# ViT tower on one core: squares of the patch embedding weighted on ACT, folded on POOL, one PE product per tile, with constants and clearing moved

## The chip, the cores and the metric

The kernel runs on 1 core of one Trainium2 chip. The metric is device time in microseconds for one execution of the whole tower. The time before is 2521.09 us, the median of 3 runs (2516.54 to 2526.69).

## What is computed

Thirty-two images of 3x112x112 become 49 patch tokens each, plus a class token, so 1600 tokens of 192 numbers. Four pairs of mixer and feed-forward layers follow (a state-space scan, attention, mixtures of experts). The change touches the tokeniser, which is a shifted-patch embedding: each patch is read together with four shifted copies, the row is layer-normalised and projected:

```python
h = _L0_tok_ref(x, L0_tok_ln_weight, L0_tok_ln_bias, L0_tok_proj_weight, L0_tok_proj_bias)
h = jnp.concatenate([jnp.broadcast_to(cls_tok, (h.shape[0], 1, h.shape[2])), h], axis=1)
h = h + _L0_attn_ref(_layernorm(h, axis=-1), ...)
```

The layer norm of a patch needs the mean and the mean square over its window, each pixel counted as often as the five copies read it (its share). The kernel gets both from matrix products over the pixels: the mean as a 193rd column of the projection, the mean square as a column of its own.

## The kernel before, in words

`embed` (from L121) works in 16 tiles of 100 tokens (two images). A tile's pixels lie as 8 chunks of 120 rows by 100 tokens. Four buffers (DEPTH = 4) hold pixels and squares in turn.

SP's queue loads three small tables, 8 chunks of shifted weights (`wshift`, L168), and then one tile of pixels after another (L176); from the fifth on, a pixel load waits until PE has finished the tile that used the buffer four tiles earlier (`multiplied`). Behind every second one of these it loads a quarter of the packed constants (L180), and the block ends with a wait for all four quarters.

DVE folds each weight chunk over its 5 shifts (L194, L198), and PE forms two bias rows from the same chunks (L267, L270). Then, for each tile, ACT squares the 800 pixels per row in one instruction (L252). PE waits for the squares, multiplies the 8 pixel chunks by the 193 folded columns (L279) and the 8 chunks of squares by the one column `share` (L282). A product in f32 shows as two instructions, so a tile has 16 and 16. DVE's `centre` (L208 to L210) takes the tile out of PSUM; after every fourth tile `variance` (L215 to L217), ACT's root and `scale` (L222, L225, L229) finish four tiles. PE may begin a tile only when `centre` of four tiles earlier has run (`stored`). POOL does nothing in this block.

`zero_spare` (from L1711) is a block of its own behind it: DVE casts two constants to bf16 (L1720, L1721), POOL clears a tile (L1725), SP stores it to the spare rows of `sums` (L1730) and waits for the store. Then `layer0_mixer` normalises (L325 and following, over DVE, POOL and ACT), projects and enters its scan (`bilinear_scan`, L558 to L675). The two bf16 constants are first used by the experts of layer 1's feed-forward. `layer1_mixer` begins with POOL copying token tiles (L1265) for PE.

Blocks follow each other: every engine ends its part before any engine begins the next block.

Of the kernel before, what the change touches and what calls it, by code (L numbers as in the profile page):

```python
# [32 lines left out]
WROWS = 120  # L33
# [31 lines left out]
class Tower:  # L65


    def __init__(self, nc, stack, args, where):
        self.nc, self.stack, self.args, self.sems, self.tensors = nc, stack, args, 0, 0
        sb = self.sbuf  # L70
        self.h = sb("h", [TILE, TILES, DIM])
        self.x = sb("x", [TILE, TILES, DIM])
        self.xT = sb("xT", [128, 2, TOKENS + 2 * TILE])
        self.psum = stack.enter_context(nc.psum_tensor("banks", [128, 8 * 512], F32))
        self.bank = [self.psum[:, 512 * i:512 * (i + 1)] for i in range(8)]
        self.old, self.theirs, self.new, self.mine = ExitStack(), [], ExitStack(), []
        self.bn = sb("bn", [TILE, TILES, 6])
        self.mv = sb("mv", [TILE, TILES, 2])
        self.loaded = self.sem("constants_loaded", lasting=True)
        self.passed = self.sem("passed", lasting=True)  # L80

        self.tables = {k: nc.dram_tensor(f"table{k}", (TOKENS, LINE + 2 * k), F32, kind="Internal").ap() for k in (2, 4)}
        self.behind = sb("behind", [TILE, TILE], dtype=BF16)
        self.every = sb("every", [TILE, 128], dtype=BF16)
        self.sums = nc.dram_tensor("sums", (TOKENS + SPARE, DIM), F32, kind="Internal").ap()
        self.consts = sb("consts", list(args["consts"].shape))
        self.w = {}
        for name, (at, shape) in where.items():
            self.w[name] = columns_of(self.consts, at, shape)

# [42 lines left out]
def embed(t):  # L133
# [4 lines left out]
    with ExitStack() as st:  # L138
# [4 lines left out]
        gain = t.sbuf("gain", [WROWS, 2, WCHUNKS, SHIFTS], st)  # L143
        share = t.sbuf("share", [WROWS, WCHUNKS], st)
        onesr = t.sbuf("onesr", [WROWS, TILE], st)
        pbias = t.sbuf("pbias", [1, DIM], st)
        rows = t.sbuf("rows", [TILE, 2, DIM], st)
        stats = t.sbuf("pstats", [TILE, TILES, 2], st)
# [7 lines left out]
        finished = t.sem("finished")  # L156
        raw, fixed = t.bank[4:4 + DEPTH], t.bank[2:4]
        args = t.args
        width = t.consts.shape[1]

        with t.block() as block:
            @block.sync
            def _(sp):
                sp.dma_start(gain[:], args["ln_gain"]).then_inc(small_in, 16)
                sp.dma_start(share[:], args["share"]).then_inc(small_in, 16)
                sp.dma_start(pbias[:], args["patch_bias"]).then_inc(small_in, 16)
                for c in range(WCHUNKS):
                    sp.dma_start(wshift[:, c], args["w_patch"][:, c]).then_inc(weights_in[c], 16)  # L168
                for n in range(TILES):
                    if n == DEPTH:  # L170
                        sp.wait_ge(rows_done, 1)
                        for image in range(2):
                            sp.dma_start(rows[SEQ * image:SEQ * image + 1, 1, :], args["cls"][0]).then_inc(cls_in, 16)
                    if n >= DEPTH:
                        sp.wait_ge(multiplied, n - DEPTH + 1)
                    sp.dma_start(pixels[:, n % DEPTH], args["pixels"][n]).then_inc(pixels_in[n % DEPTH], 16)  # L176
                    part = (n - DEPTH) // 2
                    if n >= DEPTH and n % 2 and part < CONST_PARTS:
                        at = slice(width * part // CONST_PARTS, width * (part + 1) // CONST_PARTS)
                        sp.dma_start(t.consts[:, at], args["consts"][:, at]).then_inc(t.loaded, 16)  # L180
                sp.wait_ge(t.loaded, 16 * CONST_PARTS)

            @block.vector
            def _(dve):
# [1 line left out]
                nc.vector.memset(onesr[:], 1.0).then_inc(ones_done, 1)  # L186
                one(nc.vector.memset(t.xT[0:HALF + 1, :, TOKENS:], 0.0))
                one(nc.vector.memset(t.xT[HALF:HALF + 1, :, TOKENS:], 1.0))
                dve.wait_ge(small_in, 48)
                nc.vector.tensor_copy(wsum[:, :, DIM:DIM + 1], share[:].unsqueeze(2)).then_inc(share_done, 1)  # L190

                for c in range(WCHUNKS):
# [46 lines left out]
            @block.scalar  # L239
            def _(act):  # L240
                nc.scalar.preload_act_table(ACT.Sqrt)

                def root(g):
                    at = slice(DEPTH * g, DEPTH * (g + 1))
                    act.wait_ge(var_done, g + 1)
                    nc.scalar.activation(var[:, 4, at], var[:, 3, at], ACT.Sqrt).then_inc(root_done, 1)

                for n in range(TILES):
                    act.wait_ge(pixels_in[n % DEPTH], 16 * (n // DEPTH) + 16)
                    if n >= DEPTH:  # L250
                        act.wait_ge(multiplied, n - DEPTH + 1)
                    nc.scalar.activation(squares[:, n % DEPTH], pixels[:, n % DEPTH], ACT.Square).then_inc(squared, 1)  # L252
                    if n % DEPTH == 2 and n > DEPTH:
                        root(n // DEPTH - 1)
                root(TILES // DEPTH - 1)

            @block.tensor
            def _(pe):
                pe.sem_inc(stored, DEPTH)
                pe.wait_ge(ones_done, 1)  # L260
                pe.wait_ge(small_in, 48)

                nc.tensor.matmul(fixed[1][0:TILE, 0:DIM], onesr[0:1, :], pbias[:], start=True, stop=False)
                for c in range(WCHUNKS):
                    pe.wait_ge(weights_in[c], 16)
                    for s in range(SHIFTS):
                        nc.tensor.matmul(fixed[1][0:TILE, 0:DIM], gain[:, 1, c, s:s + 1].to_broadcast([WROWS, TILE]),  # L267
                                         wshift[:, c, s, :], start=False, stop=(c == WCHUNKS - 1 and s == SHIFTS - 1))
                    pe.wait_ge(wsum_done, SHIFTS * (c + 1))
                    last = nc.tensor.matmul(fixed[0][0:TILE, 0:DIM], onesr[:], wsum[:, c, 0:DIM],  # L270
                                            start=(c == 0), stop=(c == WCHUNKS - 1))
                last.then_inc(bias_done, 1)
                pe.wait_ge(share_done, 1)
                for n in range(TILES):
                    u = n % DEPTH
                    pe.wait_ge(squared, n + 1)
                    pe.wait_ge(stored, n + 1)
                    for c in range(WCHUNKS):
                        nc.tensor.matmul(raw[u][0:TILE, 0:DIM + 1], pixels[:, u, c, :], wsum[:, c, :],  # L279
                                         start=(c == 0), stop=(c == WCHUNKS - 1))  # L280
                    for c in range(WCHUNKS):
                        last = nc.tensor.matmul(raw[u][0:TILE, DIM + 1:DIM + 2], squares[:, u, c, :],  # L282
                                                share[:, c:c + 1], start=(c == 0), stop=(c == WCHUNKS - 1))
                    last.then_inc(multiplied, 1)


# [234 lines left out]
def bilinear_scan(t, u, rate, coef, bc, direct, gain, y):  # L521
# [7 lines left out]
    with ExitStack() as st:  # L529
# [12 lines left out]
        lasts = [max(j for j in range(jobs) if group(j) == g) for g in range(2)]  # L542

        with t.block() as block:
            @block.tensor
            def _(pe):
                pe.sem_inc(summed, SLOTS)
# [694 lines left out]
def layer1_mixer(t):  # L1242

    nc, w = t.nc, t.w
    with ExitStack() as st:
# [12 lines left out]
        with t.block() as block:  # L1258
            @block.gpsimd
            def _(pool):  # L1260
                with pool.Fori(0, TILES // 2) as i:
                    for u in range(2):
                        pool.wait_ge(projected, 2 * i + u + 1)
# [442 lines left out]

def rounds(engine, times):
    return engine.Fori(0, times) if times > 1 else nullcontext(0)


def zero_spare(t):  # L1711

    nc = t.nc
    with ExitStack() as st:
        zeros = t.sbuf("zeros", [128, SUBS, DIM], st)
        zeros_done, zeroed = t.sem("zeros_done"), t.sem("zeroed")
        with t.block() as block:
            @block.vector
            def _(dve):
                nc.vector.tensor_copy(t.behind[:], t.w["behind"])  # L1720
                nc.vector.tensor_copy(t.every[:], t.w["all"])  # L1721

            @block.gpsimd
            def _(pool):
                nc.gpsimd.memset(zeros[:], 0.0).then_inc(zeros_done, 1)  # L1725

            @block.sync
            def _(sp):
                sp.wait_ge(zeros_done, 1)
                sp.dma_start(t.sums[TOKENS:TOKENS + SPARE].rearrange("(s p) d -> p s d", p=128), zeros[:]).then_inc(zeroed, 16)  # L1730
                sp.wait_ge(zeroed, 16)


def experts(t, name, src, dst, lhs, router, count, picks, func, gated, norm=None, own_gain=False, out=None, keep_sum=None, biased=False, capacity=None):
# [661 lines left out]
def tower(nc, args, out, where):  # L2396
    with ExitStack() as stack:
        t = Tower(nc, stack, args, where)
        embed(t)
        zero_spare(t)  # L2400
        layer0_mixer(t)
        layer0_ffn(t)
        layer1_mixer(t)
# [73 lines left out]
def layout(inputs):  # L2477
# [21 lines left out]
    a["w_patch"] = np.ascontiguousarray(wide[..., :DIM])  # L2499
    a["ln_gain"] = np.ascontiguousarray(wide[..., DIM:].transpose(0, 3, 1, 2))  # L2500
    a["share"] = np.ascontiguousarray((count / PATCH_DIM).astype(np.float32).reshape(WCHUNKS, WROWS).T)
    a["patch_bias"] = f["L0_tok_proj_bias"].reshape(1, DIM)
    a["cls"] = f["cls_tok"].reshape(1, 1, DIM)
    a["c_ident"] = np.eye(128, dtype=np.float32)
# [96 lines left out]
```

## Time and profile before

| | |
|---|---|
| median of 3 runs | 2521.09 us |
| the profiled execution's own time | 2526.45 us |
| its span, first to last instruction | 2524.6 us |
| mean granted TensorE clock | 0.859 |
| PE busy | 2005.6 us (79%) |
| DVE busy | 1189.0 us (47%) |
| ACT busy | 890.3 us (35%) |
| POOL busy | 843.8 us (33%) |

Times are microseconds from the span's start unless ns is written. PE is TensorE's matrix products, PEld its weight loads, which overlap with them, DVE is VectorE, ACT ScalarE, POOL GpSimd, SP the queue that issues most transfers. The engine shares are averages over stages with different limits, so a stage is read by itself: its timeline, its busy time per window, and what each engine waited for.

### The profile page before, as it was taken

Reading aid. Unit: us, or ns where it says so; the run is one execution under the profiler, and the core shown is the slowest. Engines: PE = TensorE matmul, PEld = TensorE weight load, DVE = VectorE, ACT = ScalarE, POOL = GpSimd, SP = SyncE. Lnnn points to the kernel's source line nnn. Section 1 sums busy time; section 2 is a strip of 40 time slices with the busy share of each in tenths; the row PEclk is TensorE's granted clock in tenths of the full one; section 3 lists DMA queues with packets and bytes.
Section 4 is the critical chain, followed back from the end, with each engine's and each line's share of the span. In section 5 each row is a group of like instructions: output and inputs, shape, how many; then the busy total and the mean of one; then the engine's idle time right before and its main releaser. Section 6 shows DMA issues by size and latency. Waiting matters only on the chain. (4 is left out here: it accounts for less than half of the span.)

```text
span 2524.6 us, 42132 instructions
## 1 busy us (share of the span) xinstructions
PE 2005.6 (79%) x13338; PEld 1484.1 (59%) x13338; DVE 1189.0 (47%) x2907; ACT 890.3 (35%) x1860; POOL 843.8 (33%) x759
## 2 busy tenths in 40 slices
PE   9755777987995994985995567777499938999998
PEld 8511223665764883664983222224399837999987
DVE  4348995243563113563113799998222243222222
ACT  1247784133233332342224644553222122211211
POOL 0203552012111553001552267663234312443443
PEclk9757997876896995895997789999599957999999
DMA  7100000000004871003871000000377626777774
GB/s 217 31 0 1 0 0 1 0 0 6 1 0 122 237 206 35 1 0 106 225 205 26 0 1 0 0 0 1 113 223 221 170 69 191 224 222 224 221 201 113
DMA packets 95935, 228.18 MB, mean 90 GB/s; under 512 B 22481, under 2 KB 60948, under 8 KB 87540
## 3 DMA queue, kind: packets, MB, share of 16 engines
q1 hardware_dynamic: 64564, 188.81, 23.4%
q0 software_dynamic: 31296, 38.48, 8.4%
q8 instruction: 34, 0.56, 0.1%
q14 instruction: 41, 0.34, 0.0%
HBM read 199.63 MB, written 27.62 MB: 90 GB/s over the span
## 5 line engine op out<-in xcount | busy, mean ns | idle before, releaser
L1964 PE MATMUL banks<-wt,hid 128*128 128x192 f32 x1932 | 331.7, 327 | 0.4
L1964 PEld LDWEIGHTS banks<-wt,hid 128*128 128x128 f32 x1932 | 311.8, 190 | 1.5 <-issue 0.6
L1866 POOL DMA_INDIRECT xblock<-table,take x169 | 167.6, 992 | 370.7 <-DVE gate L2149 193.8
L1939 PE MATMUL banks<-xTblock,wt 128*128 128x256 f32 (+1 forms) x1464 | 268.6, 341 | 1.7 <-ACT xTblock L2022 1.2
L2162 DVE TENSOR_TENSOR hid<-sa,banks 128x512 f32<-128x512 f32 (+1 forms) x183 | 105.9, 579 | 340.1 <-ACT sa L2043 337.3
L2043 ACT ACTIVATE sa<-banks 128x512 f32<-128x512 f32 (+1 forms) x183 | 93.3, 510 | 481.5 <-PE banks L1950 476.6
L1939 PEld LDWEIGHTS banks<-xTblock,wt 128*128 128x128 f32 x1464 | 237.6, 194 | 23.7 <-issue 1.9
L742 PE MATMUL banks<-g,consts 128*128 128x400 f32 x384 | 184.7, 571 | 60.1 <-DVE g L881 56.1
L850 POOL TENSOR_TENSOR w<-u,spreadB 128x400 f32<-128x400 f32 x192 | 192.9, 1034 | 87.0 <-ACT spreadB L821 87.0
L1871 POOL DMA_INDIRECT sums<-yblock,put x96 | 152.7, 1591 | 170.5 <-issue 98.6
L875 DVE TENSOR_TENSOR_SCAN s<-banks,w 128x400 f32<-128x400 f32 x192 | 187.7, 977 | 4.2 <-POOL w L850 4.2
L2177 DVE TENSOR_SCALAR yblock<-banks,gate 128x192 f32<-128x192 f32 x129 | 49.4, 414 | 235.2 <-PE banks L1964 204.3
L742 PEld LDWEIGHTS banks<-g,consts 128*128 128x128 f32 x384 | 61.0, 197 | 168.4 <-DVE g L881 167.2
L633 POOL TENSOR_TENSOR w<-u,r 128x400 f32<-128x400 f32 x96 | 99.0, 1033 | 175.4 <-ACT r L607 163.4
L805 ACT ACTIVATE banks<-rate,coef 128x392 f32 x192 | 113.2, 591 | 117.8 <-DVE s L875 117.8
L1950 PE MATMUL banks<-xTblock,wt 64*128 64x256 f32 (+1 forms) x1464 | 143.3, 342 | 0.0
L1871 POOL DMA_INDIRECT out<-yblock,put x65 | 103.6, 1594 | 115.0 <-issue 56.5
L1950 PEld LDWEIGHTS banks<-xTblock,wt 64*128 64x128 f32 x1464 | 116.1, 187 | 22.9 <-issue 12.1
L881 DVE TENSOR_TENSOR g<-s,banks 128x400 f32<-128x400 f32 x192 | 103.3, 540 | 0.0
L1943 PE MATMUL banks<-xTblock,wt 128*128 128x256 f32 (+1 forms) x480 | 94.7, 349 | 2.2 <-ACT xTblock L2022 1.3
L656 DVE TENSOR_TENSOR_SCAN s<-banks,w 128x400 f32<-128x400 f32 x96 | 93.8, 977 | 0.1
L1926 PE MATMUL banks<-consts,xblock 128*128 128x128 f32 x338 | 61.5, 296 | 38.7 <-DMA xblock<-table,take 38.6
(379 smaller groups left out, 3455.5 us busy)
## 6 DMA issues: line engine op xcount, KB each, us to landing
wt<-L3f_packed SPq DMA_DIRECT2D x41, 1152.0 KB, 5.6
wt<-L_packed SPq DMA_DIRECT2D x60, 576.0 KB, 4.6
wt<-L3f_packed SPq DMA_DIRECT2D x41, 576.0 KB, 5.4
wt<-L3m_packed SPq DMA_DIRECT2D x20, 1152.0 KB, 5.4
wt<-L_packed SPq DMA_DIRECT2D x20, 675.0 KB, 4.2
wt<-L3m_packed SPq DMA_DIRECT2D x20, 577.0 KB, 5.4
pixels<-pixels SPq DMA_DIRECT2D x16, 375.0 KB, 4.8
wshift<-w_patch SPq DMA_DIRECT2D x8, 450.0 KB, 11.9
```

The costliest lines, as they stand in the source:

```text
L633: nc.gpsimd.tensor_tensor(w1[:, j % SLOTS, :], u[:, group(j), at], r[:, j % SLOTS, :], ALU.mult).then_inc(w1_done, 1)
L742: nc.tensor.matmul(acc[g][0:parts, 0:CHUNK], ident[0:parts, 0:parts], g_[:, j % SLOTS, :], start=(n == 0), stop=(n == STATES - 1)).then_in ...
L805: nc.scalar.activation(rest, rate[:, g, at].rearrange("p (b t) -> p b t", t=SEQ)[:, :, 1:SEQ], ACT.Exp, scale=coef[:, g, n:n + 1]).then_in ...
L850: nc.gpsimd.tensor_tensor(w2[:, j % SLOTS, :], u[:, g, at], spreadB[:, n % 2, :], ALU.mult).then_inc(bu_done, 1)
L875: nc.vector.tensor_tensor_scan(s[:, j % SLOTS, :], decays[j % DECAYS], w2[:, j % SLOTS, :], 0.0, ALU.mult, ALU.add).then_inc(s_done, 1)
L881: nc.vector.tensor_tensor(g_[:, j % SLOTS, :], s[:, j % SLOTS, :], bankC[(j // groups) % 2][0:parts, 0:CHUNK], ALU.mult).then_inc(g_done, 1)
L1866: nc.gpsimd.indirect_dma_start(x[:, b % 2, q - column_of_block[b], :], None, table, bass.IndirectOffsetOnAxis(take[:, q:q + 1], 0)).then_i ...
L1871: nc.gpsimd.indirect_dma_start(sums, bass.IndirectOffsetOnAxis(put[:, q:q + 1], 0), y[:, b % 2, q - column_of_block[b], :], None, compute_ ...
L1939: nc.tensor.matmul(bank[:, n * j:n * (j + 1)], wt[:, v, cols(base, 2 * p + j)], xT[:, v, 0, 0:n], start=(j == 0), stop=False, skip_group_c ...
L1950: last = nc.tensor.matmul(bank[:, n * j:n * (j + 1)], wt[half, v, cols(REST_AT, 2 * p + j)], xT[half, v, 1, 0:n], start=False, stop=True, ...
L1964: last = nc.tensor.matmul(bankY[s], hid[:, m, 128 * s:128 * (s + 1)], wt[:, v, DOWN_AT + DIM * m:DOWN_AT + DIM * (m + 1)], start=(m == 0 a ...
L2162: nc.vector.tensor_tensor(hid[:, 2 * p:2 * p + 2, 0:n], sa[:, (PAIRS * v + p) % 2, 0:2 * n].rearrange("p (m n) -> p m n", m=2), second[:, ...
```

## The change

The squares are weighted before they are summed. ACT squares each chunk by itself with a scale per row, the root of `share`, so 8 instructions replace one. POOL adds the 8 weighted chunks in three halving additions (4+4 chunks, 2+2, 1+1). PE multiplies the one folded chunk by a column of ones: one product per tile in place of eight. PE now waits for the pixels ahead of the 193-column products and for POOL's sum ahead of the last one.

The clearing of spare rows goes inside `embed`, ahead of the weight loads in SP's queue; the two casts go to POOL at the start of `layer1_mixer`; the block `zero_spare` disappears. Of the constants, the first part (up to the array `first`, 737 of the columns by the arrays' shapes) is loaded behind the ninth pixel tile and awaited at the block's end; the rest is loaded in four parts behind the last pixel tile and awaited by SP in the block of `bilinear_scan`.

```diff
             def _(sp):
                 sp.dma_start(gain[:], args["ln_gain"]).then_inc(small_in, 16)
                 sp.dma_start(share[:], args["share"]).then_inc(small_in, 16)
+                sp.dma_start(root_share[:], args["root_share"]).then_inc(small_in, 16)
                 sp.dma_start(pbias[:], args["patch_bias"]).then_inc(small_in, 16)
+                sp.wait_ge(zeros_done, 1)
+                sp.dma_start(t.sums[TOKENS:TOKENS + SPARE].rearrange("(s p) d -> p s d", p=128), zeros[:]).then_inc(zeroed, 16)
...
                     if n >= DEPTH:
                         sp.wait_ge(multiplied, n - DEPTH + 1)
+                        sp.wait_ge(squared, n - DEPTH + 1)
                     sp.dma_start(pixels[:, n % DEPTH], args["pixels"][n]).then_inc(pixels_in[n % DEPTH], 16)
-                    part = (n - DEPTH) // 2
-                    if n >= DEPTH and n % 2 and part < CONST_PARTS:
-                        at = slice(width * part // CONST_PARTS, width * (part + 1) // CONST_PARTS)
-                        sp.dma_start(t.consts[:, at], args["consts"][:, at]).then_inc(t.loaded, 16)
-                sp.wait_ge(t.loaded, 16 * CONST_PARTS)
+                    if n == 2 * DEPTH:
+                        sp.dma_start(t.consts[:, 0:early], args["consts"][:, 0:early]).then_inc(t.loaded, 16)
+                for part in range(CONST_PARTS):
+                    at = slice(early + late * part // CONST_PARTS, early + late * (part + 1) // CONST_PARTS)
+                    sp.dma_start(t.consts[:, at], args["consts"][:, at]).then_inc(t.loaded_late, 16)
+                sp.wait_ge(t.loaded, 16)
+                sp.wait_ge(zeroed, 16)
...
                     if n >= DEPTH:
-                        act.wait_ge(multiplied, n - DEPTH + 1)
-                    nc.scalar.activation(squares[:, n % DEPTH], pixels[:, n % DEPTH], ACT.Square).then_inc(squared, 1)
+                        act.wait_ge(added_up, n - DEPTH + 1)
+                    for c in range(WCHUNKS):
+                        last = nc.scalar.activation(squares[:, n % DEPTH, c, :], pixels[:, n % DEPTH, c, :], ACT.Square, scale=root_share[:, c:c + 1])
+                    last.then_inc(squared, 1)
...
+            @block.gpsimd
+            def _(pool):
+                one = Steps(pool, pool_step)
+                nc.gpsimd.memset(zeros[:], 0.0).then_inc(zeros_done, 1)
+                for n in range(TILES):
+                    u = n % DEPTH
+                    pool.wait_ge(squared, n + 1)
+                    if n >= DEPTH:
+                        pool.wait_ge(multiplied, n - DEPTH + 1)
+                    one(nc.gpsimd.tensor_tensor(halved[:], squares[:, u, 0:4, :], squares[:, u, 4:8, :], ALU.add))
+                    one(nc.gpsimd.tensor_tensor(halved[:, 0:2, :], halved[:, 0:2, :], halved[:, 2:4, :], ALU.add))
+                    nc.gpsimd.tensor_tensor(total[:, u, :], halved[:, 0, :], halved[:, 1, :], ALU.add).then_inc(added_up, 1)
+                    pool.wait_ge(added_up, n + 1)
...
-                    pe.wait_ge(squared, n + 1)
+                    pe.wait_ge(pixels_in[u], 16 * (n // DEPTH) + 16)
                     pe.wait_ge(stored, n + 1)
...
-                    for c in range(WCHUNKS):
-                        last = nc.tensor.matmul(raw[u][0:TILE, DIM + 1:DIM + 2], squares[:, u, c, :],
-                                                share[:, c:c + 1], start=(c == 0), stop=(c == WCHUNKS - 1))
+                    pe.wait_ge(added_up, n + 1)
+                    last = nc.tensor.matmul(raw[u][0:TILE, DIM + 1:DIM + 2], total[:, u, :], onesr[:, 0:1], start=True, stop=True)
                     last.then_inc(multiplied, 1)
...
+            @block.sync
+            def _(sp):
+                sp.wait_ge(t.loaded_late, 16 * CONST_PARTS)
...
             def _(pool):
+                nc.gpsimd.tensor_copy(t.behind[:], t.w["behind"])
+                nc.gpsimd.tensor_copy(t.every[:], t.w["all"])
                 with pool.Fori(0, TILES // 2) as i:
```

## Rows read from the trace of the kernel before

**Rows 1.** Windows: stretch, busy time (instructions) per engine, PEclk, DMA share, GB/s.

```profile
25.00:90.00 65.00, 64.79 (x514) 64.70 (x512) 20.60 (x84) 12.57 (x17) 0.00 (x0) 1.00 0.51 158
```

**Rows 2.** Timeline, PE's weight loads in one tile: start, length, group.

```profile
45.19 2.56 PEld L279 LDWEIGHTS banks<-wsum,pixels 120*100 120x100 f32 x16
47.75 1.56 PEld L282 LDWEIGHTS banks<-share,squares 120*100 120x100 f32 x16
...
49.23 2.56 PEld L279 LDWEIGHTS banks<-wsum,pixels 120*100 120x100 f32 x16
```

**Rows 3.** Timeline from the last work of embed to the mixer's first.

```profile
92.90 1.13 DVE L229 BATCH_NORM_STATS2 bn<-h 100x6 f32<-100x192 f32 x4
94.30 0.42 POOL L1725 MEMSET zeros<- 128x384 f32 x1 [93.86 <-POOLq L108]
...
98.27 1.28 ACT L409 ACT_TABLE_LOAD   x1 [6.93 <-PEq L108]
```

**Rows 4.** Groups by shape, POOL's tensor-by-tensor operations: busy us, mean ns.

```profile
L850 POOL TENSOR_TENSOR w<-u,spreadB 128x400 f32<-128x400 f32 x192 | 192.9, 1034 | 87.0 <-ACT spreadB L821 87.0
...
L1394 POOL TENSOR_TENSOR h<-h,x 100x192 f32<-100x192 f32 x2 | 1.2, 592 | 9.4 <-DVE x L1628 9.4
```

**Rows 5.** Timeline, POOL additions and products beside DVE, in two later layers.

```profile
987.76 6.66 POOL L1399 TENSOR_TENSOR h<-h,wproj 100x3072 f32<-100x3072 f32 x1 [1.44 <-DMA wproj<-L_proj]
...
990.12 4.33 DVE L1591 TENSOR_SCALAR norm<-norm 100x24 f32<-100x24 f32 x1
...
1411.83 1.40 DVE L2376 SCALAR_TENSOR_TENSOR plain<-w__231,e 128x1200 f32<-128x1200 f32 x1
...
1411.99 3.81 POOL L2330 TENSOR_TENSOR u<-rate,xc 128x1200 f32<-128x1200 f32 x1 [49.90 <-DVE rate L2371]
...
1449.40 2.71 POOL L2330 TENSOR_TENSOR u<-rate,xc 128x1200 f32<-128x1200 f32 x1 [4.23 <-DVE rate L2371]
```

**Rows 6.** Groups by shape, DVE in 205 to 360 us, beside POOL's products of L633.

```profile
L662 DVE TENSOR_TENSOR g<-s,banks 128x400 f32<-128x400 f32 x77 | 43.0, 558 | 0.1
```

**Rows 7.** Timeline, the scan's start: ACT hands over to POOL.

```profile
208.33 0.52 ACT L607 ACTIVATE r<-den 128x400 f32<-128x400 f32 x1
...
209.22 2.03 POOL L633 TENSOR_TENSOR w<-u,r 128x400 f32<-128x400 f32 x2 [94.09 <-ACT r L607]
```

**Rows 8.** Groups by shape, ACT instructions with one operand per row.

```profile
L1309 ACT ACTIVATE probs<-scores,low 100x100 f32<-100x100 f32 x16 | 5.9, 370 | 9.2 <-DVE low L1329 9.2
...
L1002 ACT ACTIVATE sq<-rate,consts 128x800 f32<-128x800 f32 x4 | 3.5, 951 | 0.0
```

**Rows 9.** Timeline, the four instructions of L1002 back to back.

```profile
186.00 3.52 ACT L1002 ACTIVATE sq<-rate,consts 128x800 f32<-128x800 f32 x4
```

**Rows 10.** Timeline, the head of embed.

```profile
1.26 0.36 SPq L165 DMA_DIRECT2D share<-share  x1
...
1.96 3.67 SPq L168 DMA_DIRECT2D wshift<-w_patch  x8
...
6.36 0.32 DVE L194 TENSOR_SCALAR wsum<-wshift,gain 120x192 f32<-120x192 f32 x1 [2.97 <-DMA wshift<-w_patch]
```

**Rows 11.** DMA issues: count, KB each, median us to landing.

```profile
pixels<-pixels SPq DMA_DIRECT2D x16, 375.0 KB, 4.8
...
consts<-consts SPq DMA_DIRECT2D x2, 1337.5 KB, 8.0
```

**Rows 12.** Timeline, POOL's first work in layer 1's mixer.

```profile
526.43 0.64 POOL L1265 COPY xtile<-xT 97x200 f32 x2 [2.83 <-PEq L1269]
```

**Rows 13.** Windows in layer 1's mixer (columns as in Rows 1).

```profile
526.80:530.50 3.70, 3.67 (x19) 3.61 (x20) 0.00 (x0) 0.52 (x1) 0.27 (x1) 0.50 0.00 0
531.10:533.00 1.90, 1.90 (x19) 1.90 (x19) 0.36 (x1) 0.50 (x1) 0.35 (x1) 0.92 0.00 0
```

**Rows 14.** Timeline, the same weight loads in those two windows.

```profile
529.93 0.61 PEld L1281 LDWEIGHTS banks<-consts,xtile 96*100 96x100 f32 x2
...
532.70 0.33 PEld L1281 LDWEIGHTS banks<-consts,xtile 96*100 96x100 f32 x2
```

More of the change, by code:

```diff
@@ L79, in __init__ @@
         self.loaded = self.sem("constants_loaded", lasting=True)
+        self.loaded_late = self.sem("constants_loaded_late", lasting=True)
         self.passed = self.sem("passed", lasting=True)
@@ L86, in __init__ @@
         self.consts = sb("consts", list(args["consts"].shape))
-        self.w = {}
+        self.w, self.where = {}, where
         for name, (at, shape) in where.items():
@@ L145, in embed @@
         onesr = t.sbuf("onesr", [WROWS, TILE], st)
+        root_share = t.sbuf("root_share", [WROWS, WCHUNKS], st)
+        halved = t.sbuf("halved", [WROWS, WCHUNKS // 2, TILE], st)
+        total = t.sbuf("total", [WROWS, DEPTH, TILE], st)
+        zeros = t.sbuf("zeros", [128, SUBS, DIM], st)
+        zeros_done, zeroed, added_up, pool_step = (t.sem(n) for n in ("zeros_done", "zeroed", "added_up", "pool_step"))
         pbias = t.sbuf("pbias", [1, DIM], st)
@@ L158, in embed @@
         args = t.args
-        width = t.consts.shape[1]
+        early = t.where["first"][0]
+        late = t.consts.shape[1] - early
         with t.block() as block:
@@ L188, in _ @@
                 one(nc.vector.memset(t.xT[HALF:HALF + 1, :, TOKENS:], 1.0))
-                dve.wait_ge(small_in, 48)
+                dve.wait_ge(small_in, 64)
                 nc.vector.tensor_copy(wsum[:, :, DIM:DIM + 1], share[:].unsqueeze(2)).then_inc(share_done, 1)
@@ L249, in _ @@
                     act.wait_ge(pixels_in[n % DEPTH], 16 * (n // DEPTH) + 16)
+                    if n == 0:
+                        act.wait_ge(small_in, 64)
                     if n >= DEPTH:
-                        act.wait_ge(multiplied, n - DEPTH + 1)
-                    nc.scalar.activation(squares[:, n % DEPTH], pixels[:, n % DEPTH], ACT.Square).then_inc(squared, 1)
+                        act.wait_ge(added_up, n - DEPTH + 1)
+                    for c in range(WCHUNKS):
+                        last = nc.scalar.activation(squares[:, n % DEPTH, c, :], pixels[:, n % DEPTH, c, :], ACT.Square, scale=root_share[:, c:c + 1])
+                    last.then_inc(squared, 1)
                     if n % DEPTH == 2 and n > DEPTH:
@@ L260, in _ @@
                 pe.wait_ge(ones_done, 1)
-                pe.wait_ge(small_in, 48)
+                pe.wait_ge(small_in, 64)
                 nc.tensor.matmul(fixed[1][0:TILE, 0:DIM], onesr[0:1, :], pbias[:], start=True, stop=False)
@@ L1708, in rounds @@
     return engine.Fori(0, times) if times > 1 else nullcontext(0)
[L1711 to L1731, printed above, removed]
 def experts(t, name, src, dst, lhs, router, count, picks, func, gated, norm=None, own_gain=False, out=None, keep_sum=None, biased=False, capacity=None):
@@ L2399, in tower @@
         embed(t)
-        zero_spare(t)
         layer0_mixer(t)
@@ L2501, in layout @@
     a["share"] = np.ascontiguousarray((count / PATCH_DIM).astype(np.float32).reshape(WCHUNKS, WROWS).T)
+    a["root_share"] = np.sqrt(a["share"])
     a["patch_bias"] = f["L0_tok_proj_bias"].reshape(1, DIM)
```

## Prediction
> **What bounds the kernel now.** I read four views in this order: the page's table of engines, the windows of the first 100 us, the timeline of one tile and of the passage into the mixer, and the groups by shape for prices. The page says that PE is busiest, but the change touches only the embedding and the block behind it, so their own rows decide. While the tiles run, PE and its weight loads are busy throughout, at granted clock 1.00, while DVE has 20.60 us of work in 65, ACT 12.57 and POOL none [rows 1]. So PE sets the pace there. One tile shows its two parts: the 16 loads of the 193-column products start at 45.19, the 16 of the one-column products at 47.75, the next tile at 49.23 [rows 2]. A tile takes 4.04 us: 2.56 for the first part and 1.48 for the second, which gives just one column. Sixteen tiles take 64.6 us. DVE's last instruction of embed ends at 94.03, the clearing block begins at 94.30, the mixer at 98.27 [rows 3]: 3.97 us for a block in which no engine does much.
>
> **What PE saves.** Of the second part two loads of 16 stay: 2 x 1.48/16 = 0.19 us. The tile becomes 2.56 + 0.19 = 2.75 us, 16 tiles 44.0, so -20.6 us if PE still sets the pace. For that, ACT, POOL, DVE and the pixel ring must each need less than 2.75 us a tile.
>
> **ACT.** An instruction of 100x100 with one operand per row takes 0.370 us; four in a row of 0.951 each take 3.52 together, so each overlaps the next by 0.095 [rows 8, 9]. Eight squares: 7 x 0.275 + 0.37 = 2.3 us. That fits, with 0.45 to spare, and ACT can run up to four tiles ahead. It costs nothing; PE's products hide it.
>
> **POOL.** Additions of 400 and 192 elements took 1034 and 592 ns [rows 4]: 2.125 ns an element and 184 fixed. So 400, 200 and 100 elements take 1.03, 0.61 and 0.40 us: 2.04 a tile. Between them stand three waits of POOL on its own result, which no row shows. From below a wait costs nothing; from above it costs what ACT's handover to POOL took, 209.22 - 208.85 = 0.37 [rows 7]. A handover inside one engine should be nearer the low end: I take 0.15, so 2.5 us a tile (2.04 to 3.15).
>
> **POOL beside DVE.** The same product of 128x1200 took 2.71 us alone and 3.81 where a DVE instruction with two SBUF inputs had begun 0.16 before it; and a DVE TENSOR_SCALAR of 24 elements, begun at 990.12, ended at 994.45, just after POOL's addition ended at 994.42 [rows 5]. So whichever comes second waits out the other. DVE's products of an SBUF with a PSUM operand were not held: 558 ns beside POOL [rows 6]. In embed the two-input ones are L215, L216 and the four of L225, with L217 a TENSOR_SCALAR: 7 of the 21 DVE instructions of four tiles (84/4). Each may wait for one addition, on average 0.68 us: at most 4.8 us per four tiles on top of DVE's own 5.2 [rows 1], 10.0 in all against PE's 11.0. In return they hold POOL. If they make up some 2 of the 5.2 us, an estimate, that is 0.5 a tile at most, so POOL needs 2.5 to 3.0, PE 2.75. PE is still the likelier bound, as many of these instructions fall into POOL's pauses, but DVE will be late at the end: I take +1.5 us (0 without holds, 4.8 with all of the last four tiles' holds).
>
> The open one is L209, the negation of one element, once per tile. By the 24-element row it is held too, 16 times more; this is in the upper half of my bounds. The Trainium skill's page "GPSIMD Engine Reference", section "Specifications", limits contention to DVE instructions with two SBUF inputs or in a two-port mode. By it L209 would be held only if one element ran in such a mode, and the +1.5 would be nearer 1.0; no row tells.
>
> **The pixel ring.** A slot is refilled after `multiplied`: issue 0.3, landing 4.8 [rows 11], ACT 2.3, POOL 2.5, PE's last product 0.2 make 10.1 us against 4 x 2.75 = 11.0. It fits. The early constants (737 columns x 512 B = 0.38 MB) are as much as one pixel tile and add one such transfer in the ring's slack. SP's extra wait for `squared` is met whenever `multiplied` is.
>
> **The head.** Ahead of the weight loads SP gets two more issues, `root_share` and the store of zeros, at 0.36 each as for `share`: +0.7, and their bytes ahead of the first weight chunk. POOL clears its tile in 0.42 [rows 3] right at the start, before SP asks. DVE's folding starts on the first chunk's landing (6.36 [rows 10]) and everything up to the first tile hangs on it. I take +1.0 (0.4 if the issues overlap with the landing; 2.8 if the store adds 2 us).
>
> **The block removed, the rest.** -4.0 us; at the least -3.5 if the passage between blocks gets longer. The casts in `layer1_mixer` stand ahead of POOL's first copy, for which PE waits: two copies of 200 elements took 0.64 together [rows 12], the casts have 100 and 128, so +0.5 (0 to 0.64). The late constants, four parts of 1337 KB less 0.38 MB, about 5.1 MB, flow from the last pixel load on. At the 158 GB/s of rows 1 they take 32 us and end some 20 us into the mixer. Their wait is SP's alone, in the scan's block, which began 110 us after the mixer (208.33 against 98.27 [rows 3, 7]); SP has nothing queued behind it. Cost nothing, and if that cover went, the scan would start late by the remainder.
>
> **Sum.** -20.6 + 1.5 + 1.0 - 4.0 + 0.5 = -21.6 us. The profiled execution would go from 2526.45 to 2504.9. It lies 5.4 above the median, so the median of runs would go from 2521.1 to **2499.5 us**. Best case: -20.6 + 0 + 0.4 - 4.0 + 0 = -24.2.
>
> **Rivals.**
> *POOL becomes the bound.* At waits of 0.37 and half of the holds a tile takes 3.15 + 0.25 = 3.4 us, 16 tiles 54.4: -10.2 + 1.5 + 1.0 - 4.0 + 0.5 = -11.2, 2510; with every hold 3.65 and -7.2, 2514; at waits of 0.25 it is 2.79 + 0.25 = 3.04 and -17.0, 2504. For it: the prices lie close to PE's 2.75. Against: both must come out high, and POOL starts a tile ahead.
> *The pixels or constants are late.* If landings take 6.5 us in place of 4.8, the ring needs 11.8 per four tiles, 2.95 each, 47.2 in all: -18.4, 2503. If the mixer waited for the late constants, 10 to 20 us would come back, 2510 to 2520; nothing that it reads before the scan stands in the late part.
> *Slower: PE at its lower clock level in the tiles.* A busy PE is not enough for the higher level: in 526.8 to 530.5 it was busy 3.67 of 3.70 us at a granted 0.50 (1.2 GHz), and its weight loads took 0.61 there against 0.33 just after, at 0.92 [rows 13, 14]. At that ratio, 1.85, a tile takes 5.1 us and 16 take 81.4: +16.8 + 1.0 - 4.0 + 0.5 = +14.3, 2535. The point from which it decides is a tile of 4.2 us, where what the loop loses eats the removed block. Against it: the level held at 1.00 through all 65 us with the same 193-column products [rows 1], and what goes are the thin ones, so PE gets denser.
>
> **How the numbers follow.** PE-bound as summed 0.65; POOL the bound 0.23, about half of it short of 0.5%; late transfers 0.07; the lower clock 0.05. Half a per cent, 12.6 us, is what a measurement here can tell from no change, so faster means below 2508.5. Faster: 0.62 + 0.12 + 0.05 = 0.79; same: 0.03 (scatter of three runs) + 0.11 + 0.02 = 0.16; slower 0.05. The range goes from the best case with the scatter of the runs before (5 below their median), 2497 - 9, to the dearer POOL case, so 2488 to 2512.
>
> **What would show it.** Right: PE's weight loads start tiles 2.75 us apart, PE busy without gaps in them; embed ends near 75, and the mixer's first table load comes at 75 to 76 in place of 98.27; eight ACT instructions of about 0.37 a tile; POOL's adds at 1.03, 0.61, 0.40 and the longer ones beside L225; no later stage changed. Wrong: PE waiting for `total` in every tile (POOL the bound), ACT or PE waiting for pixels, a granted clock under 1.00 in 26 to 70, or a mixer that starts on time and loses the gain before the scan.

## The result, and the profile after

The changed kernel takes 2499.68 us (median of 4 runs, 2496.99 to 2501.28), the kernel before 2518.82 (4 runs, 2515.87 to 2526.69). The ratio is 0.9918, with a 95% interval of 0.9903 to 0.9934, so the gain is 17 to 24 us. The prediction was 2499.5, a gain of 21.6 from the earlier median of 2521.1. A second timing, beside the experiments, gave 2498.85 against 2520.14, ratio 0.9904 (0.9866 to 0.9942).

The profiled execution of the changed kernel has its own time of 2501.28 us, a span of 2499.4 and a mean granted clock of 0.86. First the timeline, cut to the lines that answer to [rows 2, 3, 7, 10], with others between them left out, as in the timelines further on (start, length, group, and in brackets the idle time before it and what ended it).

```profile
2.86 3.91 SPq L178 DMA_DIRECT2D wshift<-w_patch  x8
...
7.37 0.32 DVE L207 TENSOR_SCALAR wsum<-wshift,gain 120x192 f32<-120x192 f32 x1 [3.78 <-DMA wshift<-w_patch]
...
25.69 2.63 PEld L310 LDWEIGHTS banks<-wsum,pixels 120*100 120x100 f32 x16
25.77 1.03 POOL L283 TENSOR_TENSOR halved<-squares 120x400 f32<-120x400 f32 x1 [24.63 <-ACT squares L268]
26.88 0.61 POOL L284 TENSOR_TENSOR halved<-halved 120x200 f32<-120x200 f32 x1
27.56 0.39 POOL L285 TENSOR_TENSOR total<-halved 120x100 f32<-120x100 f32 x1
...
42.58 2.56 PEld L310 LDWEIGHTS banks<-wsum,pixels 120*100 120x100 f32 x16
44.00 2.26 ACT L268 ACTIVATE squares<-pixels,root_share 120x100 f32<-120x100 f32 x8 [1.16 <-DMA pixels<-pixels]
45.13 0.33 PEld L313 LDWEIGHTS banks<-onesr,total 120*100 120x100 f32 x2
45.38 2.56 PEld L310 LDWEIGHTS banks<-wsum,pixels 120*100 120x100 f32 x16
...
67.48 0.40 POOL L285 TENSOR_TENSOR total<-halved 120x100 f32<-120x100 f32 x1
...
70.51 0.25 PE L313 MATMUL banks<-onesr,total 120*100 120x1 f32 x2
...
72.56 1.41 DVE L238 SCALAR_TENSOR_TENSOR h<-h,pvar,rows 100x192 f32<-100x192 f32 x4
73.88 1.13 DVE L242 BATCH_NORM_STATS2 bn<-h 100x6 f32<-100x192 f32 x4
75.28 1.28 ACT L439 ACT_TABLE_LOAD   x1 [2.97 <-PEq L109]
...
182.99 1.28 ACT L627 ACT_TABLE_LOAD   x1 [12.00 <-DVE banks L674]
...
781.55 1.28 ACT L2044 ACT_TABLE_LOAD   x1
937.41 1.28 ACT L439 ACT_TABLE_LOAD   x1 [13.13 <-PEq L109]
```

Read it downwards. The first weight chunk is folded at 7.37 where it was 6.36, and the first tile's loads begin at 25.69. A tile starts 2.80 us after the one before it (42.58 to 45.38), where it was 4.04; the first part is unchanged at 2.56, and the two loads of `total` take 0.25 (45.13 to 45.38) in place of the second part. ACT's eight squares take 2.26 us together. POOL's three additions follow each other after 0.08 and 0.07 us (26.80 to 26.88, 27.49 to 27.56). DVE's last instruction of `embed` ends at 75.01 (73.88 + 1.13), and the mixer's first ACT instruction comes 0.27 later: there is no block between them any more. The mixer starts 98.27 - 75.28 = 22.99 us earlier. The scan's table load comes 182.99 - 75.28 = 107.71 us behind it. In the kernel before it stood equally far behind, as this line shows against the 98.27 of [rows 3]:

```profile
205.98 1.28 ACT L593 ACT_TABLE_LOAD   x1 [12.00 <-DVE banks L640]
```

So nothing of the gain is lost before the scan, and the new wait in its block costs nothing. The windows of the changed kernel say what PE and the transfers did (columns as in [rows 1]):

```profile
25.00:70.00 45.00, 45.00 (x290) 45.00 (x289) 26.10 (x83) 34.51 (x126) 32.81 (x48) 1.00 0.63 195
65.00:70.00 5.00, 5.00 (x34) 5.00 (x33) 3.53 (x15) 0.54 (x2) 2.05 (x3) 1.00 1.00 420
70.00:74.00 4.00, 0.77 (x7) 0.68 (x5) 2.75 (x12) 0.20 (x1) 0.00 (x0) 1.00 1.02 426
```

PE is busy through all 45 us at granted clock 1.00, so it still sets the pace, with ACT at 77% and POOL at 73% close under it. The late constants run at 420 GB/s and are nearly through by 74. Last the groups by shape of the changed kernel in 0 to 80 us, and the DVE groups of the kernel before in 25 to 94 that answer to them.

```profile
L268 ACT ACTIVATE squares<-pixels,root_share 120x100 f32<-120x100 f32 x128 | 35.8, 364 | 27.4 <-DMA pixels<-pixels 27.2
L283 POOL TENSOR_TENSOR halved<-squares 120x400 f32<-120x400 f32 x16 | 16.8, 1047 | 31.4 <-ACT squares L268 24.6 <-POOL total L285 5.3 <-issue 1.2
L284 POOL TENSOR_TENSOR halved<-halved 120x200 f32<-120x200 f32 x16 | 9.7, 608 | 1.3
L238 DVE SCALAR_TENSOR_TENSOR h<-h,pvar,rows 100x192 f32<-100x192 f32 x16 | 8.9, 616 | 0.1
L285 POOL TENSOR_TENSOR total<-halved 120x100 f32<-120x100 f32 x16 | 6.3, 395 | 1.3
L222 DVE TENSOR_SCALAR pvar<-pstats 100x1 f32<-100x1 f32 x16 | 2.5, 154 | 0.5
L228 DVE TENSOR_TENSOR pvar<-pstats 100x4 f32<-100x4 f32 x4 | 1.9, 472 | 0.0
L230 DVE TENSOR_SCALAR pvar<-pvar 100x4 f32<-100x4 f32 x4 | 1.3, 320 | 0.1
```

```profile
L225 DVE SCALAR_TENSOR_TENSOR h<-h,pvar,rows 100x192 f32<-100x192 f32 x16 | 5.6, 415 | 0.1
L209 DVE TENSOR_SCALAR pvar<-pstats 100x1 f32<-100x1 f32 x16 | 2.5, 153 | 0.6
L217 DVE TENSOR_SCALAR pvar<-pvar 100x4 f32<-100x4 f32 x4 | 0.7, 170 | 0.1
L215 DVE TENSOR_TENSOR pvar<-pstats 100x4 f32<-100x4 f32 x4 | 0.6, 156 | 0.0
```

The same DVE instructions stand in both, at other lines: 415 became 616 ns, 156 became 472, 170 became 320, and the negation of one element stayed at 153 and 154. The spans of the two profiles differ by 25.2 us while the medians differ by 19.1 and, in the second timing, 21.3. That difference is taken up with the experiments.

### The profile page after: what moved, and what is told of

Read it like the earlier page. It is cut to its first block and busy times, and to the rows that moved or that the text cites. A ratio compares the mean times of both kernels' runs of the same rounds, so it can differ in the third digit from the quotient of the medians.

```text
span 2499.4 us, 41869 instructions
## 1 busy us (share of the span) xinstructions
PE 1984.9 (79%) x13114; PEld 1463.7 (59%) x13114; DVE 1194.3 (48%) x2905; ACT 911.7 (36%) x1972; POOL 876.6 (35%) x809
## 5 line engine op out<-in xcount | busy, mean ns | idle before, releaser
L1884 POOL DMA_INDIRECT sums<-yblock,put x96 | 152.7, 1591 | 168.4 <-issue 93.4
```

The source lines that it names most:

```text
L1884: nc.gpsimd.indirect_dma_start(sums, bass.IndirectOffsetOnAxis(put[:, q:q + 1], 0), y[:, b % 2, q - column_of_block[b], :], None, compute_ ...
```

## The experiments

All are edits of the changed kernel, but the last one, which is the kernel before profiled again. To compare stages without the head, I use the stretch from the first tile's weight load to the mixer's first table load: 98.27 - 24.93 = 73.34 us before and 75.28 - 25.69 = 49.59 after.

**The squares undone** (`e2_old_squares`): ACT squares the tile in one instruction again, PE has its eight one-column products, POOL adds nothing.

```diff
-                    for c in range(WCHUNKS):
-                        last = nc.scalar.activation(squares[:, n % DEPTH, c, :], pixels[:, n % DEPTH, c, :], ACT.Square, scale=root_share[:, c:c + 1])
-                    last.then_inc(squared, 1)
+                    nc.scalar.activation(squares[:, n % DEPTH], pixels[:, n % DEPTH], ACT.Square).then_inc(squared, 1)
...
-                    pe.wait_ge(added_up, n + 1)
-                    last = nc.tensor.matmul(raw[u][0:TILE, DIM + 1:DIM + 2], total[:, u, :], onesr[:, 0:1], start=True, stop=True)
+                    pe.wait_ge(squared, n + 1)
+                    for c in range(WCHUNKS):
+                        last = nc.tensor.matmul(raw[u][0:TILE, DIM + 1:DIM + 2], squares[:, u, c, :],
+                                                share[:, c:c + 1], start=(c == 0), stop=(c == WCHUNKS - 1))
```

> Only the squares are undone: one ACT instruction per tile, no POOL adds, eight one-column products; the constants, the clearing and the waits stay as in the change. Theory (PE's products were the gain): a tile takes 4.04 us again, 16 x 1.24 = 19.8 us more, the mixer's first table load at 95.1, the whole time about 2519. Rival (the earlier constants among the pixel loads slowed the tiles, and moving them was the gain): tiles near 3 us, the mixer at 76 to 82.

It took 2512.68 us. Its timeline:

```profile
45.15 2.56 PEld L298 LDWEIGHTS banks<-wsum,pixels 120*100 120x100 f32 x16
47.70 1.56 PEld L302 LDWEIGHTS banks<-share,squares 120*100 120x100 f32 x16
49.19 0.92 PEld L298 LDWEIGHTS banks<-wsum,pixels 120*100 120x100 f32 x6
...
94.25 1.28 ACT L429 ACT_TABLE_LOAD   x1 [2.96 <-PEq L109]
```

The tile is back at 4.04 us and the mixer at 94.25. From the first tile (24.89) to the mixer it is 69.36, so the squares are worth 69.36 - 49.59 = 19.77 us, and what remains to the kernel before, 73.34 - 69.36 = 3.98, is the block. The start 0.85 earlier than forecast lies in the head, whose scatter is treated below. The whole time is 6 us under the 2519 forecast; how far a single time can be trusted is treated there too.

**The block put back** (`e1_block`): the clearing, its store and the two casts return to a block behind `embed`.

```diff
+def zero_spare(t):
...
+                nc.vector.tensor_copy(t.behind[:], t.w["behind"])
+                nc.vector.tensor_copy(t.every[:], t.w["all"])
...
+                nc.gpsimd.memset(zeros[:], 0.0).then_inc(zeros_done, 1)
...
-                sp.wait_ge(zeroed, 16)
+                sp.wait_ge(t.loaded_late, 16 * CONST_PARTS)
...
-                nc.gpsimd.tensor_copy(t.behind[:], t.w["behind"])
-                nc.gpsimd.tensor_copy(t.every[:], t.w["all"])
```

> The block of clearing and casts stands behind embed again, the store of zeros no longer ahead of the weights, the casts no longer in layer 1; the squares stay as in the change. Theory (the block cost 3.97 us by itself, the store some 0.45 at the head): tiles stay 2.80 us apart, embed's last DVE instruction ends at 74.5 in place of 75.01, the mixer's first table load comes at 78.5 to 79 in place of 75.28. If the casts on POOL cost layer 1's mixer 0.5 us, its stretch between the two table loads (84.30 us in the changed kernel) goes to 83.8; if not it stays at 84.2 or more. Rival (the block was hidden, the whole shift came from the tiles): the mixer at 75.3.

It took 2499.16 us. Its timeline:

```profile
75.49 0.42 POOL L1755 MEMSET zeros<- 128x384 f32 x1 [9.09 <-remote]
77.63 0.39 SPq L1760 DMA_DIRECT2D sums<-zeros  x1
...
80.05 1.28 ACT L435 ACT_TABLE_LOAD   x1 [9.04 <-PEq L109]
```

DVE's last instruction of `embed` ended at 73.70 here, 0.8 ahead of the forecast; that is the head again, as it lies 49.32 us behind the first tile (24.38), like the changed kernel's (75.01 - 25.69). The block brings the wait for its store back, but the mixer is later than I expected: the casts read late constants, so this kernel must wait for all of them ahead of the block, which the expectation left out. From 73.70 to 75.49 are 1.79 us, where the passage into the block took 0.27 before (94.03 to 94.30, [rows 3]), so the wait is 1.5 of them; from the clearing to the mixer it is 4.56, against 98.27 - 94.30 = 3.97. The 0.6 that this is longer by lies between the clearing and the issue of its store, 77.63 - 75.49 = 2.14 us here and 95.82 - 94.30 = 1.52 before; why was not tried. Of the casts the run says little by itself: layer 1's mixer, between its table loads, took 83.8 us here without them and 84.3 with them in the changed kernel, against 84.2 and 83.8 in the two profiles of the kernel before. The start of that stage says more. PE's first weight load there comes 0.80 us behind the stage's table load without the casts (526.83 - 526.03 in the kernel before, 508.32 - 507.52 here) and 0.88 with them (503.34 - 502.46). So they cost 0.08 us.

**All constants awaited at the end of `embed`** (`e3_await_all`):

```diff
                 sp.wait_ge(zeroed, 16)
+                sp.wait_ge(t.loaded_late, 16 * CONST_PARTS)
```

> As the changed kernel, but SP awaits the late constants too at embed's end. By the prediction's sum (5.1 MB at 158 GB/s from the last pixel load on) they would end 20 us into the mixer, so the mixer would begin at 90 or later. By the changed kernel's trace (transfers stop before the mixer begins) the wait is met: the mixer's first table load at 75.3 to 76, and waiting late saves nothing.

It took 2504.38 us. First its timeline, then one of its windows (columns as in [rows 1]):

```profile
74.85 1.13 DVE L243 BATCH_NORM_STATS2 bn<-h 100x6 f32<-100x192 f32 x4
77.60 1.28 ACT L440 ACT_TABLE_LOAD   x1 [4.33 <-PEq L109]
```

```profile
74.00:76.00 2.00, 0.00 (x0) 0.00 (x0) 1.98 (x7) 0.00 (x0) 0.00 (x0) 0.95 0.62 259
```

SP's wait for the constants stands in the view of waits as this line (us in all, how often, the longest):

```profile
SPq L195 <- DMA consts<-consts: 14.0, 1, 14.0
```

In the window of 74 to 76 the transfers run out: a DMA share of 0.62 over 2 us is the last 1.2 us of them at full share, so nearly all of them are through by 75.2, ahead of DVE's last instruction (74.85 + 1.13 = 75.98). Yet SP, whose last issue of them ended at 63.08, waited for them until 77.1. A few packets still moved up to 76.4 (10 KB in the last 0.1 us), and the wait ended 0.7 us behind the last one. The mixer starts 77.60 - 75.98 = 1.62 us behind DVE's last instruction in place of 0.27. So the later wait is worth 1.35 us. The prediction's sum said that the constants would run 20 us into the mixer, by which this kernel would have started it at 90 or later; that is refuted. The reading from the trace, 75.3 to 76, was short by 1.6, because it took the end of full traffic for the landing; and waiting late does save something.

**The additions on DVE** (`e4_dve_adds`): POOL does nothing, DVE adds two tiles ahead of PE.

```diff
+                def fold(n):
+                    u = n % DEPTH
+                    dve.wait_ge(squared, n + 1)
+                    one(nc.vector.tensor_tensor(halved[:], squares[:, u, 0:4, :], squares[:, u, 4:8, :], ALU.add))
+                    one(nc.vector.tensor_tensor(halved[:, 0:2, :], halved[:, 0:2, :], halved[:, 2:4, :], ALU.add))
+                    nc.vector.tensor_tensor(total[:, u, :], halved[:, 0, :], halved[:, 1, :], ALU.add).then_inc(added_up, 1)
+                    dve.wait_ge(added_up, n + 1)
...
+                    if n + 2 < TILES:
+                        fold(n + 2)
```

> The three additions of each tile run on DVE, two tiles ahead of its own work on the tile, and POOL only clears the zeros. Theory (PE sets the pace as long as the folding engine needs under 2.80 us a tile; DVE has 5.2 us of work per four tiles and three additions of about 0.55, 0.35 and 0.25): DVE needs some 2.5 us a tile, tiles stay at 2.80, the four long instructions of the scaling return from 0.62 to 0.415 us each, the mixer at 75.3. Rival (DVE in order, with its waits for PE and for ACT's root, falls behind): tiles of 3.0 to 3.5 us and the mixer at 78 to 86.

It took 2503.17 us; the mixer began at 75.07, 49.99 us behind the first tile. Its groups by shape:

```profile
L221 DVE TENSOR_TENSOR halved<-squares 120x400 f32<-120x400 f32 x16 | 9.1, 569 | 0.0
...
L251 DVE SCALAR_TENSOR_TENSOR h<-h,pvar,rows 100x192 f32<-100x192 f32 x16 | 5.6, 412 | 0.1
```

The addition of 400 elements takes 569 ns on DVE and 1047 on POOL, and with POOL silent the DVE instruction of 192 elements is back at 412 from 616. So the long DVE instructions of the changed kernel come from POOL's additions. Yet the stretch is 0.40 us longer, not shorter, because two tiles waited for DVE, 0.24 and 0.33 us in PE's timeline. PE is the bound either way.

**POOL made slower** (`e5_pool_extra`): the first addition is done twice.

```diff
                     one(nc.gpsimd.tensor_tensor(halved[:], squares[:, u, 0:4, :], squares[:, u, 4:8, :], ALU.add))
+                    one(nc.gpsimd.tensor_tensor(halved[:], squares[:, u, 0:4, :], squares[:, u, 4:8, :], ALU.add))
```

> POOL does the first addition of each tile twice (same result): 1.03 + 0.08 us more on a tile of 2.27, so 3.38 without holds. Theory (POOL has 0.5 us of room per tile, no more): POOL becomes the bound, tiles 3.4 us apart or, with DVE's holds, up to 3.7, granted clock still 1.00, the mixer's first table load at 75.28 + 16 x 0.6 to 0.9 = 84.9 to 89.7. Rival (POOL runs far ahead and has more room): the mixer under 80.

It took 2498.43 us. Its timeline, and one of its windows (columns as in [rows 1]):

```profile
49.16 0.25 PEld L314 LDWEIGHTS banks<-onesr,total 120*100 120x100 f32 x2 [0.65 <-POOL total L286]
...
52.55 0.25 PEld L314 LDWEIGHTS banks<-onesr,total 120*100 120x100 f32 x2 [0.67 <-POOL total L286]
...
84.85 1.28 ACT L440 ACT_TABLE_LOAD   x1 [2.96 <-PEq L109]
```

```profile
26.00:81.00 55.00, 48.86 (x291) 43.98 (x289) 28.81 (x86) 33.07 (x121) 49.01 (x64) 1.00 0.56 184
```

This is what the rival of a bound by POOL looks like: PE waits for `total` in every tile but the first, mostly some 0.65 us, a tile takes 3.4, and the mixer starts at 84.85, 58.72 us behind the first tile (26.13). One addition of 1.05 us and 0.08 of waiting more cost 58.72 - 49.59 = 9.13 us over 16 tiles, 0.57 each, so POOL had about 1.13 - 0.57 = 0.56 us to spare in a tile of 2.80. The changed kernel's own trace agrees: while squares lay ready, POOL began a tile every 2.26 us (25.77, then 28.03). The window also bears on the rival of a lower clock: with PE busy only 48.86 of 55 us the granted clock stayed at 1.00. Its total time, however, is no longer than that of the changed kernel. The last two runs say why.

**The head reordered** (`e6_head`): the store of zeros goes behind the last pixel load, `root_share` behind the weights, with a semaphore of its own.

```diff
-                sp.dma_start(root_share[:], args["root_share"]).then_inc(small_in, 16)
...
-                sp.wait_ge(zeros_done, 1)
-                sp.dma_start(t.sums[TOKENS:TOKENS + SPARE].rearrange("(s p) d -> p s d", p=128), zeros[:]).then_inc(zeroed, 16)
                 for c in range(WCHUNKS):
                     sp.dma_start(wshift[:, c], args["w_patch"][:, c]).then_inc(weights_in[c], 16)
+                sp.dma_start(root_share[:], args["root_share"]).then_inc(root_in, 16)
...
+                sp.wait_ge(zeros_done, 1)
+                sp.dma_start(t.sums[TOKENS:TOKENS + SPARE].rearrange("(s p) d -> p s d", p=128), zeros[:]).then_inc(zeroed, 16)
```

> The store of zeros moves behind the last pixel load, the load of root_share behind the weights; all else as in the change. Theory (the two issues ahead of the weights cost 0.76 us at the head): the first folding on DVE at 6.5 to 6.6 in place of 7.37, the first tile's loads at 24.9 to 25.0 in place of 25.69, the mixer at 74.5; the whole time 0.8 us less, under what the timing can tell. Rival (the store at the end is awaited): the mixer at 75.3 or later.

Its timeline:

```profile
1.95 3.67 SPq L176 DMA_DIRECT2D wshift<-w_patch  x8
6.32 0.32 DVE L208 TENSOR_SCALAR wsum<-wshift,gain 120x192 f32<-120x192 f32 x1 [3.15 <-DMA wshift<-w_patch]
24.60 2.63 PEld L311 LDWEIGHTS banks<-wsum,pixels 120*100 120x100 f32 x16
```

The weights are asked for at 1.95 us again in place of 2.86, and the first fold and the first tile follow 1.05 and 1.09 earlier than in the changed kernel's first profile, some 0.3 earlier than I expected. The mixer began at 74.19, 49.59 us behind the first tile as in the changed kernel, so the wait for the store at the end costs nothing. The time is 2499.06 us (median of 4, 2491.32 to 2503.26), ratio to the kernel before 0.9917 (0.9892 to 0.9941). One microsecond can't be told from the changed kernel's time in that, so it is shown in the stage and not in the total.

**Both kernels again** (`e7_changed_again`, `e8_before_again`): no edit.

> The changed kernel once more, unchanged, to see what of the differences is the program and what is scatter. Theory (the stages up to the mixer repeat, the three stages of the sparse experts in layers 1 to 3 vary by some microseconds from run to run): tiles 2.80 us apart, the mixer's first table load at 75.0 to 76.6 (the head varies with the store of zeros), the expert stages each between 151 and 162 us and not at the values of the first profile (155.9, 156.3, 158.4). Rival (each program has its own fixed expert times, set by when it reaches them): the same three values within 0.5 us.

> The kernel before once more. Theory as for the changed kernel: the mixer at 98.2 to 98.4, the scan's table load 107.7 us behind it, the three expert stages anywhere in 151 to 162 us (first profile 160.9, 155.5, 153.3). Rival: the same three values within 0.5 us.

The timelines of the changed kernel, then of the kernel before, each again:

```profile
74.71 1.28 ACT L439 ACT_TABLE_LOAD   x1 [2.97 <-PEq L109]
780.18 1.28 ACT L2044 ACT_TABLE_LOAD   x1
944.80 1.28 ACT L439 ACT_TABLE_LOAD   x1 [13.13 <-PEq L109]
```

```profile
23.41 2.63 PEld L279 LDWEIGHTS banks<-wsum,pixels 120*100 120x100 f32 x16
...
96.76 1.28 ACT L409 ACT_TABLE_LOAD   x1 [6.93 <-PEq L108]
```

One stretch repeats, the head and some later stages do not. The stretch from the first tile to the mixer repeats: 96.76 - 23.41 = 73.35 before (73.34 the first time), and 49.73 after (49.59). The head scatters: the first tile of the kernel before starts at 24.93 and 23.41, which is why my 98.2 to 98.4 for its mixer was missed, and the changed kernel's 75.0 to 76.6 by 0.3. And the experts of layer 1's feed-forward, whose code the change does not touch, take 944.80 - 780.18 = 164.6 us in one profile of the changed kernel and 937.41 - 781.55 = 155.9 in the other; I had expected at most 162. The rival of fixed values per program is refuted by that. Three stretches between ACT table loads vary in this way: layer 1's experts (from the load at 781.55 in the changed kernel), the attention of layer 2's mixer and the experts of layer 2's feed-forward. In sum they hold about half of what the two profiles of one kernel differ by, 4.0 of 8.2 us before and 1.9 of 3.9 after. In us, with the span and what is left of it without the three:

| kernel | the three stretches | span | the rest |
|---|---|---|---|
| before | 160.9, 155.5, 153.3 | 2524.6 | 2054.9 |
| before, again | 154.3, 155.4, 156.0 | 2516.4 | 2050.7 |
| squares undone | 154.4, 155.4, 152.7 | 2510.8 | 2048.3 |
| POOL made slower | 155.9, 151.0, 152.1 | 2496.4 | 2037.4 |
| block put back | 155.9, 154.0, 152.5 | 2497.2 | 2034.8 |
| all constants awaited | 161.2, 155.2, 152.6 | 2502.5 | 2033.5 |
| changed, again | 164.6, 155.3, 152.6 | 2503.3 | 2030.8 |
| additions on DVE | 161.5, 157.8, 153.0 | 2501.3 | 2029.0 |
| changed | 155.9, 156.3, 158.4 | 2499.4 | 2028.8 |
| head reordered | 161.0, 155.1, 153.8 | 2497.8 | 2027.9 |

Without the three stretches the kernels stand almost in the order in which their mixers start, and the two profiles of before lie 23.0 us above the two of after (2052.8 and 2029.8 in the mean). With them, the two profiles of before differ by 8.2 us. The kernel with POOL made slower, whose mixer starts 9.6 us late, has a short time in its one profile because its three stretches are 11.6 us shorter in sum than those of the changed kernel's first profile, while the rest is 8.6 longer. That this is scatter is not shown: it was profiled once, and the sums of the repeated kernels moved by less. What makes these stretches vary was not tried and stays open.

## Why the prediction was right

The likeliest case came true: PE sets the pace of the tiles, at a shorter period. Step by step:

**PE's tile.** Predicted 2.75 us and -20.6; measured 2.80, and 16 x (4.04 - 2.80) = 19.8; undoing the squares alone gave 19.77. The two remaining loads cost 0.25 and not the 0.19 of two sixteenths: the time of the second part does not divide evenly.

**ACT and POOL.** ACT needs 2.26 us for its eight squares, the 2.3 predicted. POOL's prices were right (1.03, 0.61 and 0.40 predicted; 1047, 608 and 395 ns measured); its wait on itself is 0.08 and not 0.15, so that it needs 2.26 us a tile with the handover, not 2.5. The rival of a bound by POOL was sound but some 0.5 us away, as the doubled addition showed.

**POOL and DVE holding each other.** This term was mis-sized. The mechanism is there on DVE's side and the cost is not. The DVE instructions with two SBUF inputs grew as predicted, and with the additions on DVE they shrank again. But the +1.5 us at the end is wrong: POOL had finished its last addition at 67.88 (67.48 + 0.40), while PE's last product ended at 70.76 (70.51 + 0.25), so nothing held the last four tiles' work on DVE: the four instructions that begin at 72.56 take 1.41 us together, not four times 0.616. Nor did the holds slow POOL, for which I had allowed up to 0.5 us a tile: of its 16 additions of 400 elements the median took 1038 ns and the longest 1157. Of the one-element negation, which I had left open, the rows decide: 153 and 154 ns, not held. By the Trainium skill, page "GPSIMD Engine Reference", section "Specifications", contention is limited to DVE instructions with two SBUF inputs or in a two-port mode; the trace agrees for the two-input instructions (415 to 616 and 156 to 472 ns). The TENSOR_SCALAR of four elements went from 170 to 320 ns; it has one tensor input, like the one of one element that was not held, and no run here shows in which mode either ran.

**The head.** Predicted +1.0 (0.4 to 2.8). The first profiles show 25.69 - 24.93 = 0.76; moving the store and the small table away gave 1.09. Over all profiles the first tile starts at 25.57 in the mean with the store ahead of the weights (six) and at 24.33 without it (four), so about +1.2, beside a scatter of 1.5 to 1.8. DVE's first fold tells it with less scatter: 6.32 to 6.36 in the three without the store and `root_share`, 6.86 with `root_share` alone (`e1_block`), 7.23 to 8.04 in the six with both.

**The block.** Predicted -4.0, measured -3.98.

**The casts.** Predicted +0.5 (0 to 0.64). At PE's first weight load of the stage they cost 0.08: POOL's first copy came 0.40 us behind the table load before as well (526.43 against 526.03), and the casts fit almost wholly into that. The term took their length for their cost.

**The late constants.** This step failed, without harm to the sum, as its term was nothing either way. I took the 158 GB/s of [rows 1] for what the transfers can do and let them run 20 us into the mixer. That row is the traffic that the tiles asked for, at a DMA share of 0.51. With nothing else to wait for, they ran at 420 GB/s and share 1.00, and the wait moved to the scan is worth 1.35 us, where I had counted on its hiding much more.

Up to the mixer the prediction's terms give -20.6 + 1.5 + 1.0 - 4.0 = -22.1, the trace -22.99. The +1.5 that did not come and the tiles that gained 0.8 less partly cancel, and the head came out 0.2 less in this pair. The total of -21.6 lies inside the interval of the timings; that it met the median within 0.2 us is luck, as single runs of either kernel spread over several microseconds.

The slower rival, PE at its lower clock level, did not occur: the granted clock was 1.00 (2.4 GHz) in all tiles, and also where PE was left waiting in each tile.

## What to carry to other kernels

A product with one output column still costs all its weight loads, so where PE sets the pace, sums that other engines can do in the shadow are worth moving: here 1.24 us a tile, though ACT and POOL then have only some half a microsecond to spare. Read a transfer rate beside its DMA share before using it as a price: an average at share 0.51 says what was asked for, not what can be had. And when one stage is to be judged, measure it between two fixed events in both traces; here it repeats within 0.15 us, while the spans of two profiles of one kernel differ by 4 and 8. And do not take the end of full traffic for the landing: here the wait ended 1.9 us later.

## What the runs showed that I had not expected

The constants ran at 420 to 426 GB/s at a full DMA share, while the weights and pixels at the head ran at 230 at nearly the same share, in this window of the kernel before:

```profile
10.00:12.00 2.00, 2.00 (x8) 1.78 (x7) 1.86 (x6) 0.00 (x0) 0.00 (x0) 1.00 0.98 230
```

The weights come in 120 rows of 3.75 KB a chunk (450.0 KB), the constants in longer rows; whether that is the cause was not tried.

DVE instructions of four elements per row were held beside POOL's additions (156 to 472 ns) no less than those of 192 (415 to 616), so the price of such a hold did not shrink with the DVE instruction. And the additions are about twice as fast on DVE (569 against 1047 ns). The Trainium skill states this too, on the page "GPSIMD Engine Reference", section "Engine selection", where it gives elementwise additions to VectorE. Yet the time to the mixer did not get shorter by it, 49.99 against 49.59 us, because PE set the pace in both.
